# Moving a quarter of the softmax sums' reciprocal behind the step's maxima on VectorE

## What is computed

```
def ffn(x):  return x @ ternary(weight).T + bias
def attn(x):
    k, q, v = split(x @ Wqkv + bqkv)
    s = einsum('bsnh,btnh->bnst', q, k) / sqrt(32), causal mask
    return (softmax(s) @ v) @ Wo + bo
x = x + 0.5 * ffn(layernorm(x))
x = x + attn(layernorm(x))
x = x + 0.5 * ffn(layernorm(x))
```

## Time and profile before

| | |
|---|---|
| median of 3 runs | 1316.94 us (1316.63 to 1317.14) |
| the profiled execution | 1315.88 us |
| its span, first to last instruction | 1313.7 us |
| granted clock of TensorE, mean | 0.977 of full |
| TensorE matmul busy | 94% |
| VectorE busy | 63% |
| ScalarE busy | 38% |
| GpSimd busy | 27% |

### The profile page before, as it was taken

The page is one execution under the profiler, slowest core; times in us unless marked ns, Lnnn a source line. Parts: engine busy times, 40 slices in busy tenths (PEclk is TensorE's granted clock), DMA queues, the critical chain, the costliest instruction groups (busy, mean ns, idle before and its releaser), DMA issues.

```text
span 1313.7 us, 27193 instructions
## 1 busy us (share of the span) xinstructions
PE 1235.4 (94%) x10938; PEld 749.1 (57%) x10938; DVE 832.7 (63%) x2048; ACT 501.9 (38%) x1139; POOL 348.2 (27%) x492
## 2 busy tenths in 40 slices
PE   4689999999999999999999999999999999998886
PEld 3466554555666565655656565655656566654454
DVE  6764556688545667689645767679644666655444
ACT  1222434344434334343433434344443434334421
POOL 4821110245001222236100322336201222300233
PEclk8898999999999999999999999999999999989988
DMA  7422201011103001321102102311102102000110
GB/s 240 145 81 80 83 34 59 26 63 44 42 2 130 18 34 49 114 82 49 50 1 99 49 10 74 113 66 58 41 18 73 58 26 74 26 10 10 42 49 32
DMA packets 40685, 77.26 MB, mean 59 GB/s; under 512 B 5232, under 2 KB 10352, under 8 KB 40560
## 3 DMA queue, kind: packets, MB, share of 16 engines
q1 hardware_dynamic: 40560, 75.52, 17.0%
HBM read 49.81 MB, written 25.17 MB: 57 GB/s over the span
## 4 chain that ended last, share of the span: by engine, by line
PE 84%; DVE 9%; issue 3%; POOL 2%; ACT 2%; DMA 1%; SPq 0%; DVEq 0%; ACTq 0%; POOLq 0%
PE bank L964 28%; PE bank L1024 11%; PE bank L1046 11%; PE bank L1068 10%; PE bank L1079 9%; PE bank L989 8%; PE bank L981 3%; PE bank L1052 3%; DVE mst L741 2%; DVE st L701 1%; DVE hn L712 1%; ACT prob L897 1%; DVE junk L747 1%; DVE xt L732 1%; POOL rstd L617 1%
## 5 line engine op out<-in xcount | busy, mean ns | idle before, releaser
L897 ACT ACTIVATE prob<-bank 128x512 f32<-128x512 f32 (+3 forms) x768 | 314.6, 497 | 311.2 <-PE bank L1052 310.7
L747 DVE CUSTOM_DVE_ANT_0 junk<-bank,mask 128x384 bf16<-128x384 f32 (+3 forms) x512 | 220.4, 487 | 144.4 <-PE bank L1024 143.8
L741 DVE TENSOR_REDUCE mst<-bank 128x1 f32<-128x512 f32 x256 | 159.0, 684 | 121.0 <-PE bank L1024 121.0
L1046 PE MATMUL bank<-qT,kT 32*128 32x512 f32 (+2 forms) x2304 | 190.8, 384 | 11.2 <-DVE mst L741 5.9
L652 POOL TENSOR_SCALAR_AFFINE_SELECT prob<-prob 128x512 f32<-128x512 f32 x128 | 81.3, 635 | 446.2 <-ACT prob L897 446.1
L964 PE MATMUL bank<-hT,wqk 128*128 128x512 f32 x768 | 194.4, 402 | 0.0
L1024 PE MATMUL bank<-kT,qT 32*128 32x512 f32 (+2 forms) x2304 | 182.1, 383 | 4.2 <-DVE mst L741 1.7
L1024 PEld LDWEIGHTS bank<-kT,qT 32*128 32x128 f32 x2304 | 103.0, 184 | 135.7 <-issue 94.8
L964 PEld LDWEIGHTS bank<-hT,wqk 128*128 128x128 f32 x768 | 141.1, 190 | 38.3 <-issue 7.6
L1079 PE MATMUL bank<-prob,ones 128*32 128x512 f32 (+3 forms) x1536 | 160.3, 489 | 0.0
L1046 PEld LDWEIGHTS bank<-qT,kT 32*128 32x128 f32 x2304 | 105.8, 184 | 93.6 <-issue 45.6
(11 more groups left out here) (76 smaller groups left out, 1096.4 us busy)
## 6 DMA issues: line engine op xcount, KB each, us to landing
wqk<-weight_scratch SPq DMA_DIRECT2D x30, 512.0 KB, 3.3
wvo<-weight_scratch SPq DMA_DIRECT2D x20, 512.0 KB, 6.0
xt<-in_L_attn_x_dram SPq DMA_DIRECT2D x32, 256.0 KB, 3.7
residual_scratch<-xt SPq DMA_DIRECT2D x32, 256.0 KB, 2.0
xt<-residual_scratch SPq DMA_DIRECT2D x32, 256.0 KB, 3.6
out_dram<-xt SPq DMA_DIRECT2D x32, 256.0 KB, 2.0
o<-in_L_attn_Wqkv_dram SPq DMA_DIRECT2D x12, 256.0 KB, 4.6
weight_scratch<-o SPq DMA_DIRECT2D x6, 512.0 KB, 3.0
```

Source lines behind the costliest of these rows:

```text
L741: nc.vector.tensor_reduce(mst[:, 1, at:at + 1], psum(u, h), AX, ALU.max).then_inc(ring_free, 1)
L747: nc.vector.tensor_tensor_reduce(junk[:, turn % 2, 0:n], psum(u, h)[:, 0:n], mask[:, CW - n:CW], 1.0, -3e38, ALU.add, ALU.max, mst[:, 2 * ...
L897: nc.scalar.activation(prob[:, at % 2, h, off:CW], psum(("S", b, n), h)[:, off:CW], ACT.Exp, scale=SCALE)\
L1046: nc.tensor.matmul(psum(u, h)[:, off:CW], kT[g % 2][row, x, P * kb:P * kb + P], qT[g % 2][row, y, CW * c + off:CW * c + CW], start=(term = ...
```

## The change

In VectorE's slot the quarter's reciprocal, and the product that closes a chunk, go from ahead of `normal` to behind the maxima (`s.blocks`), ahead of the whole uses. In slots with no maxima that is where they were. `uses()` is blocks and then whole, so the order of all else is as before.

```
                 if k == 0:
                     feedforward_weights()
+                for u in NORMALISED[k]:
+                    normal(u)
+                for u in s.blocks:
+                    use(u)
                 if s.b < B:
                     inversions(s)
-                for u in NORMALISED[k]:
-                    normal(u)
-                for u in s.uses():
+                for u in s.whole:
                     use(u)
                 for u in s.uses():
                     if u[0] in ("F1", "O"):
```

## The result

The changed kernel takes **1325.15 us** (median of 5 runs, 1322.93 to 1326.87) against 1316.94 us (5 runs, 1316.17 to 1319.59) of the kernel before on the same chip: ratio 1.0059, interval [1.0043, 1.0075]. It is slower by 0.6%. Its profiled execution took 1322.93 us, with a span of 1321.0 us and a mean granted clock of 0.983 (before 0.977).

> The changed kernel again, beside the others on one chip. By group lengths I expect the profile of the first run again within 0.1 us where the clock is full: groups 0 +1.9, groups 1 +1.0, group 2 +1.2 against before; by the clock's low stretches the time may be 1323 to 1333.

The account below looks back on a forecast made before the run. TensorE, busy 94% of the span, was taken as the bound. Terms 4.8 + 2.1 + 3.4 = 10.3 us on the profiled 1315.9 gave 1326.2; with the median 1.1 us above, 1327.2 us, range 1318 to 1338.

Parts of the forecast that it names:

- Maxima earlier: Outside group 2, maxima gain nothing by going ahead of the reciprocal, since VectorE waits for A before them in nearly every step.
- lows of P and M later: Low halves behind the moved reciprocal come up to 0.93 us later; taken as zero, bounds 0 to 0.2 us per group.
- Step 4, groups with nothing after A: Late product delays ACT's sums evacuation, PE's sums and step 5's A: 1.3 or 1.7 us a group, 4.8 us in all.
- the trade that the prediction described: Batch 1, group 0: if the low clock goes, half of its 3.5 us is won and 1.5 us paid, near zero.
- Group 1: Batches 1 to 3, F2.2 follows A in step 4 and hides part of ACT's delay: 0.7 us each, 2.1 in all.
- Group 3: Batches 0 to 2, a projection in step 4 makes A come late enough to cover ACT's delay: zero.
- Group 2: Batches 0 to 2, VectorE is full and waits are exchanged: 1.45 us late each, 3.4 us in all after batch 0's gain.
- All four parts: Group 2: 1.38 us `hn` wait goes; VectorE idles 1.2 us; step 5's `hn` comes late; S of steps 7, 9 waits.
- The sum: Whole kernel: 4.8 + 2.1 + 3.4 = 10.3 us slower.
- The clock rival: New hold-ups in 9 groups; if six lower the clock for 3.5 us, +10 us, 1337 us; chance 0.14.
- The faster rival: Group 2: reciprocal before `hn` was the price, 3.0 us of waits in each of three groups; 1310.5 us, chance 0.10.
- The port rule: Step 4: two-SBUF-input products and GpSimd lock each other out; up to 14 us if all 14 met, by rows unchanged.

Follow-up runs that it names:

- with only step 4 put back: The changed kernel, but in step 4 of every group reciprocal and product ahead of the maxima as before; 1314.93 us against 1320.55 for the kernel before.
- the repeat: The changed kernel, unaltered, measured a second time beside the experiments: 1327.02 us against 1317.22 for the kernel before, ratio 1.0077.
- with two tiles: The changed kernel with two `rec` tiles used in turn, so evacuation waits for the product of the chunk before the last; 1315.02 us against 1320.55 before.
- the run with `hn` first: The kernel before, with reciprocal and product moved behind the normalisation but still ahead of the maxima, in all steps; 1313.72 us against 1320.55 before.
- the run with group 2 as before: The changed kernel, with the change in groups 0, 1 and 3 only and group 2 in the old order; 1329.10 us against 1320.55 before.

## Why the prediction was right

The forecast was 1327.2 us in a range of 1318 to 1338; 1325.15 came, slower, as forecast. By its steps:

- **Maxima earlier, worth nothing; lows of P and M later, free.** Right but for 0.1 us a group: with only step 4 put back, groups 0 and 1 have their old lengths to 0.1 us, and that 0.1 is in step 9. (Of the products 15 move in step 8, not 16: the last group has no maxima there.)
- **Step 4, groups with nothing after A.** Forecast 1.3, 1.7 and 1.7; measured +1.34, +1.87, +1.87. The parts fit too: the sums started 1.23 us later, forecast 1.26 (by its own rows, 727.93 less 726.71, 1.22), and A's row was 0.56 us longer, forecast 0.45. The last 0.1 is step 9's. Batch 1 group 0 came at +0.2 against 0.1, by the trade that the prediction described: its low clock went, and the hold came. Batch 3 group 2, forecast 0, fell by 1.5 where 3.4 us of its low clock went; where all of it went, in the repeat, it took 62.6 us, and 61.3 with step 4 put back, so the hold of 1.3 is there too.
- **Group 1.** Forecast 0.7 each; measured 0.97, 1.12 and 1.07. The term was too small by a third. Step 5 grew by 0.89 in batch 1: its T came at 502.94 on the old time scale (505.42, less the 2.48 by which the step begins later), where the prediction's chain gave 502.8 and its sum took 0.7 for the difference of 0.76. The sums started 0.39 us later, which its own 500.54 says (they began at 500.16 before), but which it never priced. The rest, again, is step 9's 0.1.
- **Group 3.** Forecast 0, measured 0.1 or less.
- **Group 2.** Forecast 1.45; measured +1.19 at full clock. All four parts came: 1.38 gone, VectorE idle for ACT (1.21 us forecast as 1.2), step 5 late (a wait of 1.31), S of steps 7 and 9 held by `hT` (0.66 and 1.51, forecast over 1 each). The way there differed: batch 1 was 0.8 us late at the start of step 6, 0.6 at that of step 8, 0.4 early at that of step 9 and 1.2 late at that of step 10, where the forecast has 0.5 to 0.7, 0.9, 0.1 late and 1.45. And the runs correct what I called the loss: I summed the holds of steps 7 and 9. They are there with two tiles as well, 2.2 us, and the group is no longer than before, since `hn` first in step 4 pays for them. What the change *costs* there beyond that trade is VectorE's idle time of 1.2 us in step 4.
- **The sum.** At full clock the changed groups lose 1.3 + 3.7 + 3.2 + 0.5 (b0g2) + 2.4 (group 2 twice, by batch 1's row) = 11.1 us, where the sum had 10.2 for them. The profile shows 7.3 because about 15 us less ran at the low clock. That is the one step that I had wrong in kind: I took the clock as it was in the profile before, or as worse. So it is partly luck that 1325.15 lies only 2 us from the forecast: group 1 cost 1.1 us more than its term and group 2 less, and by the clock alone the time may move by more than these 2 us, as the repeat shows (+9.8 against before, where the first set had +8.2 and the forecast +10.3).
- **The clock rival** (1337) did not appear in this set of runs, nor the Trainium skill's rule that I had put beside it (TensorE: Matmul & The Clock Gate, "What's actually happening", a gate closed by default) as a reason for more low clock: there was less. In the repeat, with a profile of mean clock 0.973, low stretches of 3.4 us did come in step 5 of three groups 0; batch 2's lasted 73.8 us instead of 73.6, since PE was waiting there anyhow.
- **The faster rival** fell by its own point: it wanted `hT`'s low half before S asks for its fourth bank, and S waits 0.66 and 1.51 us for it.
- **The port rule.** No product of step 4 met GpSimd, as forecast, and they took 691 ns. Whether it holds was shown elsewhere, by the run with `hn` first: 1.59 us beside GpSimd. The product began 0.25 us after GpSimd's addition and ended 0.55 us after it. The rule of the Trainium skill (SBUF — State Buffer, "SBUF: two separate sides"), that the one which starts first holds the port pair, agrees with this.

What I expected of the first experiments in absolute time was off by 2 to 7 us each, and by up to 8 against the kernel before beside it; the groups at full clock came as expected or near it, the low clock did not. What stays open is which hold-ups bring the low clock. The hold of 1.38 us in step 4 of group 2 was followed by it in some groups of the kernel before and in all three of the run with group 2 as before, but other holds of over 1 us (the sums' wait of 1.04 us in step 5 of the changed kernel's groups 0) were followed by it in one profile and not in the next. With two tiles, where the 1.38 us are gone, it came in step 9 of two groups 2, where S is held for 1.5 us. I found no rule in these runs, and tried none on purpose.

## What to carry to other kernels

Price a moved instruction by everybody who waits for its result, and by what stands behind that waiter in its queue: 1.6 us of VectorE work moved within its slot, where it was free for VectorE, held ACT 3.1 us and PE 1 to 2 us, because one tile had to be read before it could be refilled. A second tile takes the price away, and is worth nothing where nobody waits. On an engine that is full over several steps no order tried here helped (with the same instructions in it, batches 1 and 2's group 2 lasted 80.1 to 81.4 us at full clock); find work in it that may be done where the engine is idle, here 3.5 us for each such group.

## What the runs showed of the hardware

- The same kernel takes 1312 to 1324 us over 44 runs on three chips, and most of that spread goes with TensorE's granted clock: within a chip the span has a standard deviation of 2.5 to 3.3 us, span times mean granted clock one of 1.4 to 2.2. A change of 0.4%, as of three kernels here that came out "faster" by their medians, can be no more than that; the lengths of stretches at full clock repeat to 0.1 us and tell it.
- A low stretch costs half its length only where PE had work: step 5 of batch 1, group 0 took 9.85 us with 3.4 us of it before and 8.26 without (with two tiles), but in the changed kernel, where it falls into a wait, 10.20 and 10.04. Over the groups 0 it cost 0.0 to 0.3 us there.
- A product of two tiles of SBUF on VectorE took 1.59 and 1.70 us where it started behind a GpSimd instruction of 1.29 us, and 0.69 alone. Where a product falls in time can thus be worth more than its own length.
